# Separate rows for messages in the two edge layers of a graph network kernel

## What is computed

```python
x_ = jnp.concatenate([h[src], h[dst], e], axis=1)          # layer 0
m = jax.nn.relu(x_ @ W1 + b1) @ W2 + b2
h_new = jax.ops.segment_sum(m, dst, num_segments=h.shape[0])
...
msg = jax.nn.relu(x[src] + edge_attr @ We + be)            # layer 1
aggr = jax.ops.segment_sum(msg, dst, num_segments=x.shape[0])
```

## Time and profile before

| | us |
|---|---|
| median of 3 runs | 3221.57 (3219.41 to 3228.64) |
| the profiled execution, its own time | 3219.47 |
| its span, first to last instruction | 3217.6 |
| edge loop of layer 0, additions L865 at 154.6 to 1107.8 | 90 periods of 10.59 |
| edge loop of layer 1, additions L865 at 1204.6 to 2135.8 | 93 periods of 10.01 |
| first product of the propagation, L1648 | from 2263.95 |
| TensorE / VectorE / ScalarE / GpSimd busy | 87% / 56% / 12% / 38% |

### The profile page before, as it was taken

The page is one execution under the profiler, slowest core; times in us unless marked ns, Lnnn a source line. Parts: engine busy times, 40 slices in busy tenths (PEclk is TensorE's granted clock), DMA queues, the critical chain, the costliest instruction groups (busy, mean ns, idle before and its releaser), DMA issues.

```text
span 3217.6 us, 59952 instructions
## 1 busy us (share of the span) xinstructions
PE 2784.3 (87%) x18663; PEld 1846.7 (57%) x18663; DVE 1789.8 (56%) x3704; ACT 397.3 (12%) x871; POOL 1209.1 (38%) x1431
## 2 busy tenths in 40 slices
PE   6788888988888858888888888885899999999998
PEld 5577777777777746666666666664333333333333
DVE  4666666666666657777677776674865111111113
ACT  2111111111111111111111111111001000000000
POOL 4455555555555525555555555550000000000000
PEclk9999989899989979999999999996899999999999
DMA  4122222222212122222222222220899999999998
GB/s 116 26 49 46 49 46 49 47 47 49 47 36 46 46 56 61 60 60 60 60 60 60 60 60 60 60 59 4 316 363 343 332 346 348 351 351 354 349 353 277
DMA packets 376594, 447.30 MB, mean 139 GB/s; under 512 B 154575, under 2 KB 193589, under 8 KB 373290
## 3 DMA queue, kind: packets, MB, share of 16 engines
q1 hardware_dynamic: 323834, 376.76, 36.0%
q0 software_dynamic: 38784, 39.79, 6.4%
q10 hardware_dynamic: 13920, 30.00, 2.5%
HBM read 416.03 MB, written 30.36 MB: 139 GB/s over the span
## 4 chain that ended last, share of the span: by engine, by line
PE 50%; issue 14%; another core or an unknown queue 11%; DVE 10%; SPq 9%; DVEq 3%; DMA 1%; ACT 1%; ACTq 0%
PE bank L1648 26%; PE bank L1468 10%; PE bank L1491 4%; SPq L518 3%; PE bank L1455 2%; SPq L521 2%; PE bank L1480 2%; PE bank L1621 2%; DVE arena L865 1%; SPq L509 1%; DVE arena L815 1%; PE bank L1652 1%; DVE arena L805 1%; DVEq L858 1%
## 5 line engine op out<-in xcount | busy, mean ns | idle before, releaser
L1468 PE MATMUL bank<-arena 128*128 128x320 bf16 x6090 | 889.4, 302 | 57.3 <-DVE arena L815 42.8
L1648 PE MATMUL bank<-arena 128*64 128x512 f32 (+1 forms) x4368 | 891.2, 543 | 35.4 <-DVE arena L1067 33.3
L1468 PEld LDWEIGHTS bank<-arena 128*128 128x128 bf16 x6090 | 595.9, 99 | 320.6 <-DVE arena L815 58.4
L651 POOL DMA_INDIRECT arena<-d_p,arena x606 | 577.6, 953 | 488.0 <-PE bank L1480 332.3
L651 POOL DMA_INDIRECT arena<-d_t,arena x606 | 577.6, 953 | 418.2 <-PE bank L1480 260.5
L1648 PEld LDWEIGHTS bank<-arena 128*64 128x64 f32 x4368 | 316.5, 136 | 521.8 <-issue 465.7
L822 DVE SCALAR_TENSOR_TENSOR bank<-arena,bank 128x320 f32<-128x320 f32 x404 | 206.1, 553 | 581.0 <-remote 427.9
L1480 PE MATMUL bank<-arena 128*65 128x47 f32 x3232 | 269.2, 233 | 203.3 <-issue 198.2
L1491 PE MATMUL bank<-arena 128*128 128x150 f32 x2352 | 398.7, 327 | 0.0
L1491 PEld LDWEIGHTS bank<-arena 128*128 128x128 f32 x2352 | 384.7, 223 | 6.9
L1480 PEld LDWEIGHTS bank<-arena 128*65 128x65 f32 x3232 | 242.8, 140 | 248.9 <-issue 238.8
(11 more groups left out here) (200 smaller groups left out, 1628.1 us busy)
## 6 DMA issues: line engine op xcount, KB each, us to landing
arena<-d_w SPq DMA_DIRECT2D x312, 1024.0 KB, 8.5
arena<-d_code SPq DMA_DIRECT2D x203, 128.0 KB
d_w<-arena ACTq DMA_DIRECT2D x24, 1024.0 KB
arena<-in_edge_attr SPq DMA_DIRECT2D x101, 128.0 KB
arena<-d_p,arena POOLq DMA_INDIRECT x606
arena<-d_t,arena POOLq DMA_INDIRECT x606
arena<-d_rec SPq DMA_DIRECT2D x588, 4.0 KB
arena<-d_q SPq DMA_DIRECT2D x202, 11.8 KB
```

Source lines behind the costliest of these rows:

```text
L651: g.indirect_dma_start(G[:, b, j, 0:F], None, table, bass.IndirectOffsetOnAxis(ap=idx[:, b, j:j + 1], axis=0)).then_inc(r.g[b], 16)
L1468: last = t.matmul(psY[g], SOH[:, g, a_, :], X[:, a_, z, :, :], start=a_ == z == 0, stop=a_ == SLICES - 1 and z == PARTS - 1)
L1648: last = t.matmul(banks[t_ % 4][F * (n % 2):F * (n % 2) + F, 0:w_], old[:, n, :], right, start=n < 2, stop=False)
```

## The change

Messages get a buffer `M` of their own with rows of FM = F + 1 = 65 values, and `G` shrinks to 64. The addition reads `G` and writes `M`; ReLU and segment sums work on `M`; the weight column moves there. GpSimd now waits for `r.add[b]` (raised by the addition of i - 2) and no longer for `r.seg[b]`. What has to be kept in order goes to VectorE: before the addition writes `M[:, b]` it waits for `r.seg[b]` (segment sums of i - 2), and before `select` writes columns 6 and 7 of `G[:, b]` it waits for `r.add[b]`. GpSimd still copies its index columns, after waiting for the landing of the gathers of i - 2 (`r.g[b]`). Behind layer 1's loop GpSimd waits for the last gathers and sums before it clears `accL`. To make room, the weights `w1ab` move into the place of `G` (they are read before the first gather) and a small area shrinks.

```diff
-FG = 80
+FM = F + 1
@@ arena
-        o_g = take(2 * 8 * FG)
+        o_g = take(2 * 8 * F)
+        o_m = take(2 * 8 * FM)
...
-        G = at(o_g, 2, 8, FG)
+        G = at(o_g, 2, 8, F)
+        M = at(o_m, 2, 8, FM)
+        w1ab = at(o_g, P)
@@ gpsimd, superblock
-                pool.wait_ge(r.seg[b], h + 1)
+                pool.wait_ge(r.add[b], h + 1)
@@ gpsimd, behind layer 1
+            def ordered1():
+                edge_loop(pool, 1, superblock)
+                for b in range(2):
+                    pool.wait_ge(R[1].g[b], 16 * TILES[b][0] * (NSB // 2 + 1 - b))
+                    pool.wait_ge(R[1].agg[b], NSB // 2 + 1 - b + 1)
@@ vector, one_hots
-                beside = OH[:, b][:, :, SPAN:SPAN + 1] if r is R[0] else G[:, b, :, F:F + 1]
+                beside = OH[:, b][:, :, SPAN:SPAN + 1] if r is R[0] else M[:, b, :, F:F + 1]
@@ vector, select
+                v.wait_ge(r.add[b], h + 1)
                 for z, tile in enumerate(TILES[b]):
@@ vector, superblock
-                rows_ = G[:, b, :, 0:F]
-                d.tensor_tensor(rows_, psPre.rearrange("p (k f) -> p k f", f=F), rows_, ALU.add).then_inc(r.add[b], 1)
+                v.wait_ge(r.seg[b], h + 1)
+                d.tensor_tensor(M[:, b, :, 0:F], psPre.rearrange("p (k f) -> p k f", f=F), G[:, b], ALU.add).then_inc(r.add[b], 1)
@@ scalar, superblock
-                rows_ = G[:, b, :, 0:F]
+                rows_ = M[:, b, :, 0:F]
@@ tensor, superblock
-                    last = t.matmul(psSeg[0:F + 1, 64 * b:64 * b + SPAN], G[:, b, j, 0:F + 1], OH[:, b, j, 0:SPAN],
+                    last = t.matmul(psSeg[0:F + 1, 64 * b:64 * b + SPAN], M[:, b, j, :], OH[:, b, j, 0:SPAN],
```

More of the change, by code:

```diff
@@ L126, in build @@
         o_ident = take(P)
-        o_w1ab = take(P)
         o_w2 = take(HALF)
@@ L130, in build @@
         o_hi1 = take(PT * NB)
-        o_small = take(111)
+        o_small = take(32)
         o_lo = top[0]
@@ L136, in build @@
         ident = at(o_ident, P)
-        w1ab = at(o_w1ab, P)
         w2p = at(o_w2, HALF)
@@ L142, in build @@
         first = at(o_small + 1, 6, parts=WQ)
[L143 to L146, removed]
+        wcols0 = at(o_small + 7, PW * WIN)
+        first2 = at(o_small + 25, 2)
+        flag = at(o_small + 27, 1, parts=1).bitcast(i32)
+        worst = at(o_small + 28, 1, parts=1)
         onesM = ones.to_broadcast([P, P])
@@ L679, in _ @@
             pool.wait_ge(s.st_t1, 16)
-            by_order(pool, lambda: general(R[1]), lambda: edge_loop(pool, 1, superblock))
+            def ordered1():
[3 more added lines that the diff above has]
+                    pool.wait_ge(R[1].agg[b], NSB // 2 + 1 - b + 1)
+            by_order(pool, lambda: general(R[1]), ordered1)
             g.memset(accL, 0.0).then_inc(s.consts, 1)
@@ L883, in ordered0 @@
                 for b in range(2):
-                    prep(d.memset(G[:, b, :, F:F + 1], 1.0))
+                    prep(d.memset(M[:, b, :, F:F + 1], 1.0))
                 prep(d.tensor_copy(qtab, qtab0))
```

## The result

| | us |
|---|---|
| before, median of 4 runs | 3221.99 (3219.41 to 3228.64) |
| changed kernel, median of 4 runs | 3819.81 (3807.19 to 3821.62) |
| ratio | 1.184, 95% interval 1.181 to 1.188 |
| profiled execution of the changed kernel, its own time and its span | 3807.19, 3805.2 |
| mean granted clock of TensorE, before and after | 0.948, 0.886 |

What follows compares the result with a forecast made beforehand. It took the loop of gather batch, hold of TensorE's signals, segment sums and next batch as the bound. Layer 0 39 us less and layer 1 16 us more made -23 us, from 3219.5 to 3196 us; range 3095 to 3385.

Steps and rivals of the forecast that it cites:

- The batch's start: GpSimd's next batch of six gathers starts 1.42 us after the addition's start, where it was 6.63.
- The end of the hold: TensorE's held instructions and signals all move again 8.66 us after a batch's first gather call.
- the hold: Towards the end of each gather batch TensorE's instructions and signals are held; the trace shows when it ends, not its cause.
- Where the segment sums end: TensorE's segment sums end 2.96 us after the batch's first call, following source rows that end at 1.87.
- Which side of the hold that is: The segment sums' signal at 2.96 us passes; the products' at 4.07 is held until 8.66.
- 12.9 us a superblock, 3700: Segment sums' signal held too, VectorE's 2.68 us chain after it; priced at 3300 for the mean; earlier-hold rivals' chance 0.28.
- Layer 0: Forecast 10.18 us a superblock, 39 us less in all; 12.1 and 147 us more if the transposes' signal is held.
- TensorE's loss of pace: Source rows: 4 of 30 matmuls done by 8.66 us, the rest by 12.4; loop still closes, 0.3 us of slack used.
- Layout, new waits, the moved `w1ab`: Each put at 0; uncertainty 10 us both ways for row layout, up to 19 us for VectorE's added waits.
- The port: Rival: gather calls beside VectorE work slowed to 1.69 us by a shared SBUF port; over 3550 us, chance 0.02.
- The doubt that I named last: The whole argument fails if the hold is tied not to the batch but to something beside it today.
- my loop: Batch, hold, products' signal, addition, next batch: 8.66 + 0.1 + 0.68 + 0.74 = 10.18 us in both layers; chance 0.38.

## Why the prediction was wrong, step by step

**The batch's start** was right: 1522.32 to 1523.74 is the 1.42 us of the sum, and the wait is for the addition.

**The end of the hold** was right: I put 8.66 us after the first call, and L883 came at 8.76, one semaphore's way behind.

**Where the segment sums end** was right: 2.96 foreseen, 2.81 measured.

**Which side of the hold that is** was the step that failed. From a signal at 1.74 that passed and one at 4.4 that didn't I took it that one at 2.96 passes. It doesn't: in the rows shown here signals of segment sums at 2.81 and 3.61 and of a source tile at 3.93 were all late, and of 91 signals of segment sums that the trace records in layer 1's loop, sent 2.3 to 5.6 us into a batch, none arrived less than 3.0 us after the sums' end. That one reading swung the sum from 10.18 to 12.9 us a superblock. I had that case among the rivals, "12.9 us a superblock, 3700", with the right chain of 2.68 us behind the hold (2.76 measured), and then argued it away with "partial holds are likelier than full ones" to a mean of 3300. No row said so. The range's upper end of 3385 followed from it; with the rival at its own price it would have been 3700, still 107 us below the run that was profiled.

**Layer 0** was mis-sized even in that rival: the source rows' signal was held too (14.08 us), because TensorE, let go only at the end of a batch, had transposes, products and the pair to do before the next source rows.

**TensorE's loss of pace** I had put inside the hold, 4 of 30 source-row matmuls. In layer 1 they started ahead of the batch instead, by 2.44 us in the superblock shown above and by 2.55 in the one below, and the trace shows no wait between two of them; their loss was the clock: the granted clock fell to 0.886 in the mean. Where TensorE had idled for 3.58 us the 30 matmuls took 6.95 us, at the lower level of the clock (1.2 GHz) until 1513.78 and at 2.4 GHz from there; after 2.67 us of idling, in the superblock shown above, 4.32 us, at 2.4 GHz throughout:

```profile
1508.28 6.95 PE L1475 MATMUL bank<-arena 128*128 128x320 bf16 x30 [3.58 <-DVE arena L821]
...
1510.83 0.97 POOL L652 DMA_INDIRECT arena<-d_t,arena  x1 [5.63 <-DVE arena L872]
...
1515.07 1.09 PE L1487 MATMUL bank<-arena 128*65 128x47 f32 x16
1515.38 0.56 DVE L829 SCALAR_TENSOR_TENSOR bank<-arena,bank 128x320 f32<-128x320 f32 x1 [2.22 <-PE bank L1475]
...
1519.63 0.20 DVE L883 TENSOR_TENSOR arena<-bank,arena 65x47 f32 x1 [2.91 <-remote]
```

The period stayed at 12.9 in both superblocks, since VectorE waits for the hold anyway. These rows show one thing more. The second source tile ends at 1508.28 + 6.95 = 1515.23, 4.40 into the batch of 1510.83, and is taken 0.15 later; the segment sums right behind it end at 1516.16, 5.33 into it, and wait 3.47 us. So not every signal in the stretch is held.

**Layout, new waits, the moved `w1ab`** at 0 were right, by the run with the layout alone: 1.0009.

**The port** was rightly given little: a gather call took 0.948 us in the first group above, and 0.953 in the earlier trace rows. The Trainium skill, SBUF — State Buffer, section "Who interferes with whom", has VectorE and GpSimd exclude each other on a shared port in certain modes and with certain operands. By that rule the calls would have got longer only if the change had put them beside such work of VectorE, and as the prediction says, the loops have none but the small copy; the calls' length agrees.

**The doubt that I named last**, that the hold might not be tied to the batch, is answered: without calls it is gone, with three it is shorter, and with a batch moved it moves. But the trace of one chip couldn't show that others don't have it. On C and D nothing is held, so my loop doesn't exist there; on D the change is worth 0.2%, on C it was not run.

## What to carry to other kernels

When a row shows that something is held until a moment, count every signal that the change moves into that stretch as caught until a row shows one that passed as late; between a passing and a held neighbour the costly side deserves its full price in the range. A wait that seems to delay a queue for nothing can be what keeps two sensitive stretches apart: here GpSimd's wait for the segment sums put the batch just behind the signal that VectorE needs most. Before tuning such a phase, run on more than one chip: the same kernel took 2803 and 3222 us.

## What the runs showed of the hardware

- Six indirect gathers of 128 rows, 1.25 us apart, held TensorE's signals and instructions, and no signals of VectorE or ScalarE, on chips A, B, E and that of the first comparison, which may be one of them (before: 3177 to 3222 us), and nothing on C and D (2803 and 2804 us). Whether it is the chip or its condition at the time, and what differs, stays open.
- In the changed kernel's layer 1 loop the signals of segment sums that the trace records (91) were sent by sums that ended 2.3 to 5.6 us into a batch, and arrived 7.2 to 8.8 us into it; with three calls they arrived at 2.9 to 4.4. Signals of source tiles that ended 3 to 4.6 into it arrived 2.3 us late at most. What decides within the stretch is open.
- Plain transfers by GpSimd or ScalarE to the same places, 3.2 us a batch, held nothing on a chip where indirect ones do; three indirect calls, 3.5 us a batch, did hold, on another such chip. 64 rows a call held as long as 128.
- Two batches that touch hold TensorE through both: one or two matmuls in 0.7 us for some 9 us.
- GpSimd was busy 38% of the time in the kernel before, and its gathers were worth 434 of 3177 us, most of it through the hold (some 370, as an estimate from the 2803 us of chips C and D).
